# The broadcast matmul of B in a Mamba stage contracts over 128 rows in place of 64

## The chip, the cores and the metric

One core of a Trainium2 chip runs the whole program. The metric is the device time in microseconds (us) of one execution. The kernel before took 3117.87 us (median of 3 runs, 3114.83 to 3124.79).

## The reference, cut to what matters

The model is a chain of residual blocks on `x` of shape (4, 1024, 128), float32: a mixture of experts, a Mamba block, the same mixture again, a ternary feed-forward, an attention, the ternary again. Only the Mamba block is touched. Each of its two directions computes

```python
xz = h @ in_proj_w.T
x, z = (xz[..., :D_INNER], xz[..., D_INNER:])
x = jax.nn.silu(_causal_depthwise_conv(x, conv_w, conv_b))
x_dbl = x @ x_proj_w.T
dt = jax.nn.softplus(x_dbl[..., :DT_RANK] @ dt_proj_w.T + dt_proj_b)
Bm = x_dbl[..., DT_RANK:DT_RANK + D_STATE]
Cm = x_dbl[..., DT_RANK + D_STATE:]
dA = jnp.exp(dt[..., None] * A)
dBx = (dt * x)[..., None] * Bm[:, :, None, :]
h = dA_t * h + dBx_t            # step by step in time
y = jnp.einsum('bdn,bn->bd', h, C_t)
```

with D_INNER = 256 channels and D_STATE = 16 states. For each state n, one row of Bm (a value for each time step) is needed on all 128 partitions, since it multiplies `dt * x` of every channel.

## The kernel before, in words

The function `mamba` works in 16 blocks `b` of 512 time steps: 4 sequences, 2 directions, 2 halves of a sequence. A block has 16 steps `v`, one for each state, and each step handles two halves `h` of 128 channels, so 512 pairs (called G) in all. For one pair:

- ACT makes `dA` = exp(dt * A) (line 1446), in a ring of 8.
- PE makes `Bp`, the row of B of this state on all partitions, once for the two halves (`rows`, line 1276). The stationary operand is `sel[:, v, :]`, zeros and ones that pick the row, and the moving operand is `bcs`, which holds B and C in 64 rows: rows 0 to 31 the part that was rounded off, rows 32 to 63 the rounded value, both float32r. So the matmul contracts over 64 rows. `Bp` is a ring of 3 PSUM banks, and a bank is free again when the scans of its step are done.
- DVE multiplies `u` = dt * x by `Bp` (line 1551) and runs the scan (line 1527) into `H`.
- POOL multiplies `H` by C (`cb`, which a DMA brings) into `hc` (line 1634), a ring of 8.
- PE adds `hc` into `Y` by a matmul with the identity in float32 (line 1339, two instructions for each pair).

Each engine has its own list of instructions, written out in this order. On PE a step `v` issues `rows(b, v + 2)`, then at most one of the projections that use the bank `O` (`o_use`: T transposes at 1288, x at 1294 to 1296, which is 12 matmuls, z at 1299 to 1301, xp at 1305, dt at 1309, out at 1314), then `add_y(b, v - 1)`. `uses_of` says which projection comes at which step. At `v = 1` `add_y` also opens `Y` for the block (`open_y`, lines 1329 and 1331). The projections of a block prepare the next or the one after it: dt goes over ACT (`softplus`) and POOL (lines 1660, 1656, 1651) to `u` (line 1645), which DVE needs at the first product of a block.

Before the scans, in block -1, DVE copies the selection matrix to `sel` (line 1589) out of `dA`, where a DMA put it, and then normalizes the second group of rows (line 1497). PE waits for `s_pre` before the first `rows`.

Of the kernel before, what the change touches and what calls it, by code (L numbers as in the profile page):

```python
# [8 lines left out]
F32R = mybir.dt.float32r  # L9
ACT = mybir.ActivationFunctionType  # L10
ALU = mybir.AluOpType
AX = mybir.AxisListType.X

P = 128
# [3 lines left out]
BLK = 512  # L18
# [5 lines left out]
def wait(eng, sem, value):  # L24

    if not isinstance(value, int) or value > 0:
        eng.wait_ge(sem, value)
# [18 lines left out]
class Phase:  # L46
# [5 lines left out]
    def sb(self, name, shape, dt=F32):  # L52
        return self.ctx.enter_context(self.nc.sbuf_tensor(f"{self.tag}_{name}", shape, dt))
# [4 lines left out]
    def sem(self, name):  # L58
        s = self.ctx.enter_context(self.nc.semaphore(f"{self.tag}_{name}"))
        self.sems.append(s)  # L60
        return s
# [1028 lines left out]
def mamba(nc, tag, x, ident, w, back):  # L1090

    NS = 16
    DBC = 2 * 2 * NS
# [8 lines left out]
    RING = 4  # L1102
# [5 lines left out]
    def place(b):  # L1108

        return b // 4, (0, 0, 1, 1)[b % 4], (0, 1, 1, 0)[b % 4]  # L1110

    def has_scan(b):
        return 0 <= b < NB
# [40 lines left out]
    def through(what, b, v):  # L1154

        return sum(k in COUNTED[what] for bb, vv, k in ORDER if (bb, vv) <= (b, v))

    def slot_of(b, lag, kind):

        use = lambda v: uses_of(b).get(v - lag)  # L1160
        return lambda v: use(v) if use(v) and use(v)[0] == kind else None

    with ExitStack() as ctx:
        ph = Phase(nc, ctx, tag)
        sb, sem = ph.sb, ph.sem
# [5 lines left out]
        dtw = sb("dtw", [DBL, 2, HALF, P])  # L1171
        alog, aneg = sb("alog", [P, 2, HALF, NS]), sb("aneg", [P, 2, HALF, NS])
        wo = sb("wo", [P, HALF, P])
        sel = sb("sel", [DBC, NS, P], F32R)
        mhalf, one, mone = sb("mhalf", [P, TILES]), sb("one", [P, 1]), sb("mone", [P, 1])
        pads = sb("pads", [P, PADW])
        stats, mv = sb("stats", [P, TILES, 6]), sb("mv", [P, TILES, 2])
# [3 lines left out]
        zs = sb("zs", [P, HALF, NCH, BLK])  # L1181
        xs = sb("xs", [P, 4, HALF, BLK])
        dbl = sb("dbl", [DBL, 2, BLK])
        bcs = sb("bcs", [DBC, 4, BLK], F32R)
        dt, u = sb("dt", [P, 2, HALF, BLK]), sb("u", [P, 2, HALF, BLK])
        ROUNDS = UB // RING
        HW = BLK + ROUNDS
# [1 line left out]
        H, hc = sb("H", [P, RING, HW]), sb("hc", [P, HCRING, BLK])  # L1189
# [11 lines left out]
        O = ph.ps("O", [P, BLK])  # L1201
# [4 lines left out]
        s_cst, s_aexp, s_wh, s_wc, s_wl, s_pre = (sem(n) for n in ("cst", "aexp", "wh", "wc", "wl", "pre"))  # L1206
# [4 lines left out]
        s_O, s_Od, s_Oa = sem("O"), sem("Od"), sem("Oa")  # L1211
# [2 lines left out]
        s_ab, s_ee, s_uu, s_ln, s_um = sem("ab"), sem("ee"), sem("uu"), sem("ln"), sem("um")  # L1214
        s_sr, s_co = sem("sr"), sem("co")
        s_dt, s_u = sem("dt"), sem("u")
        s_B = sem("B")
        s_cb = [sem(f"cb{r}") for r in range(RING)]
        s_dA, s_bx, s_scan = sem("dA"), sem("bx"), sem("scan")
# [11 lines left out]
        sels = dA[0:DBC, 0:RING, :].rearrange("p a (n c) -> p (a n) c", c=P)  # L1231
# [15 lines left out]
        def padded(c, shift=0):  # L1247
            return slice(PADW + c * BLK + shift, PADW + (c + 1) * BLK + shift)

        with nc.Block() as block:  # L1250
# [16 lines left out]
            def _(pe):  # L1267
                def rows(b, v):

                    Q = b * NS + v  # L1270
                    if Q >= NB * NS:
                        return
                    if Q % NS == 0:
                        pe.wait_ge(s_bcs, Q // NS + 1)
                    wait(pe, s_scan, 2 * (Q - BRING) + 2)
                    pe.matmul(Bp[:, Q % BRING, :], sel[:, Q % NS, :], bcs[:, Q // NS % 4, :], start=True, stop=True)\  # L1276
                      .then_inc(s_B, 1)

# [86 lines left out]
            def _(act):  # L1365
# [13 lines left out]
                def o_read(b, v, use):  # L1379
                    kind, part, tb = use  # L1380
                    i, e, c = place(tb)
                    if kind == "out":
                        return
                    act.wait_ge(s_O, through("O", b, v))
                    if kind == "T":
                        act.activation(xh[:, padded(c)], O[:], ACT.Copy).then_inc(s_xh, 1)
                    elif kind == "x":
                        act.activation(xs[:, tb % 4, part, :], O[:], ACT.Copy).then_inc(s_Oa, 1)
                    elif kind == "z":
                        wait(act, s_g, 4 * i)  # L1390
                        act.activation(zs[:, part, c, :], O[:], ACT.Copy).then_inc(s_Oa, 1)
                    elif kind == "xp":
                        wait(act, s_crow, 16 * tb)
                        act.activation(dbl[:, tb % 2, :], O[0:DBL, :], ACT.Copy).then_inc(s_dbl, 1)
                        act.activation(bcs[:, tb % 4, :], O[0:DBC, :], ACT.Copy).then_inc(s_Oa, 1)
                    else:
                        m = 2 * tb + part
                        bias = vecs[:, 1, e, part:part + 1]
                        act.activation(ab[:], O[:], ACT.Abs, bias=bias).then_inc(s_ab, 1)
                        wait(act, s_dt, m - 1)  # L1400
                        act.activation(rl[:, part, :], O[:], ACT.Relu, bias=bias).then_inc(s_Oa, 1)
# [74 lines left out]
            def _(dve):  # L1476
                ch = Chain(dve, s_gch)

                def returned(b):
                    back.combine(dve, ring, s_read, x, b, ch)  # L1480
# [28 lines left out]
                def product(G):  # L1509
                    return bx[:, G // 2 % 2, :] if G % 2 == 0 else Bp[:, G // 2 % BRING, :]  # L1510
# [29 lines left out]
                for b in range(-1, NB + 1):  # L1540
                    uses = uses_of(b)
                    for v in range(NS):
                        if has_scan(b):
                            for h in range(HALF):
                                G = b * UB + 2 * v + h
                                dve.wait_ge(s_B, b * NS + v + 1)
                                if G == UB:
                                    scan(G - 1)
                                if G % UB == 0:
                                    dve.wait_ge(s_u, 2 * (b + 1))  # L1550
                                dve.tensor_tensor(product(G), u[:, b % 2, h, :], Bp[:, G // 2 % BRING, :],  # L1551
                                                  ALU.mult).then_inc(s_bx, 1)
                                if G not in (0, UB):
                                    scan(G - 1)
                            if G == NB * UB - 1:
                                scan(G)
                        if (b, v) in RETURNS:
                            n, group = RETURNS[b, v]
                            returned(n)
                            if group:  # L1560
                                statistics(GROUPS[group])
                        if v == 1 and b > 0 and (b - 1) % 4 in (2, 3):
                            gate(b - 1)
                        if b > 0 and slot_of(b, -2, "T")(v):
                            normalize(uses[v + 2][2])
                        if slot_of(b, 2, "T")(v):
                            c = place(uses[v - 2][2])[2]
                            dve.wait_ge(s_xh, through("D", b, v - 2) - sum(
                                k == "out" for bb, vv, k in ORDER if (bb, vv) <= (b, v - 2)))
                            dve.tensor_tensor(xl[:, padded(c)], O[:], xh[:, padded(c)].bitcast(F32), ALU.subtract)\  # L1570
                               .then_inc(s_Od, 1)
                        if slot_of(b, 2, "out")(v):
                            i, _, c = place(uses[v - 2][2])
                            dve.wait_ge(s_O, through("O", b, v - 2))
                            xb = x[:, i * SEQ + c * BLK:i * SEQ + (c + 1) * BLK]
                            dve.tensor_tensor(xb, xb, O[:], ALU.add).then_inc(s_Od, 1)
                        if (b, v) == (-1, 3):
                            returned(1)
                            statistics(GROUPS[1])
                            dve.wait_ge(s_ld, 16 * len(LOADS))  # L1580
                            for e in range(2):
                                for h in range(HALF):
                                    last = dve.tensor_scalar(diag[:, e, h, :], ident[:], vecs[:, 2, e, h:h + 1], None,
                                                             ALU.mult)
                            last.then_inc(s_pre, 1)
                            dve.wait_ge(s_aexp, 1)
                            dve.tensor_scalar(aneg[:], aneg[:], -1.0, None, ALU.mult).then_inc(s_pre, 1)
                            dve.wait_ge(s_sel, 16)
                            dve.tensor_copy(sel[:], sels).then_inc(s_pre, 1)
                            normalize(1)  # L1590

            @block.gpsimd
# [822 lines left out]
```

## Time and profile before

| | |
|---|---|
| median of 3 timed runs | 3117.87 us |
| lowest and highest | 3114.83 and 3124.79 us |
| the profiled execution, span from first to last instruction | 3183.4 us |
| PE / weight loads / DVE / ACT / POOL busy over the span | 83% / 53% / 74% / 55% / 45% |

The profiled execution is slower than the timed ones: its span alone is 65.5 us, or 2.1%, over their median. The page of the profile has no time for the same execution outside the span. The scans of the Mamba block run from about 395 to 1425 us of the span. PEld in a row is the load of weights into the array, and PE the matmul itself. A shape such as 64\*128 in a row of PE is rows times columns of the array that the instruction uses.

### The profile page before, as it was taken

The numbers are of one execution on the slowest core, as the hardware profiler recorded it, in microseconds if no ns is written. First come the engines' busy times: TensorE is split into PE (matmuls) and PEld (weight loads), VectorE is DVE, ScalarE is ACT, GpSimd is POOL, SyncE is SP. The second block draws the span as 40 slices with busy tenths as digits, with TensorE's granted clock in tenths as the row PEclk, the third lists the DMA queues.
The fourth block names the chain that finished last, engine by engine and source line by source line (L and its number), as shares of the span: only waits on it lengthen the run. The fifth ranks groups of instructions, "written<-read, shape, count | busy, mean of one in ns | idle before, by whom it ended". The sixth has DMA issues, their size and how long they took to land. (4 is left out here: it accounts for less than half of the span.)

```text
span 3183.4 us, 38531 instructions
## 1 busy us (share of the span) xinstructions
PE 2649.1 (83%) x11128; PEld 1684.0 (53%) x11128; DVE 2342.8 (74%) x4109; ACT 1746.4 (55%) x3003; POOL 1430.6 (45%) x1514
## 2 busy tenths in 40 slices
PE   6888378889889989867888589949888889885999
PEld 5666233333334334225766467736555556553877
DVE  6688279989999999987688544477878777764444
ACT  3467365546556646523566345536776667763554
POOL 2465578888878878863464440031211111110000
PEclk9899688989899989996899789969999999996999
DMA  2146222222222222211146200000000000001000
GB/s 66 34 131 133 76 62 64 70 64 72 64 70 72 72 67 70 73 57 54 36 134 115 66 26 1 0 12 1 1 1 2 2 1 1 1 1 37 7 7 13
DMA packets 99373, 146.10 MB, mean 46 GB/s; under 512 B 12892, under 2 KB 50524, under 8 KB 98980
## 3 DMA queue, kind: packets, MB, share of 16 engines
q1 hardware_dynamic: 82052, 98.41, 10.5%
q0 software_dynamic: 16608, 44.78, 6.4%
q8 instruction: 91, 1.49, 0.2%
q14 instruction: 110, 0.90, 0.1%
q10 hardware_dynamic: 512, 0.53, 0.1%
HBM read 124.78 MB, written 18.87 MB: 45 GB/s over the span
## 5 line engine op out<-in xcount | busy, mean ns | idle before, releaser
L1634 POOL TENSOR_TENSOR a_hc<-a_H,a_cb 128x512 f32<-128x512 f32 x512 | 622.4, 1226 | 191.0 <-DVE a_H L1527 160.5
L1339 PE MATMUL a_Y<-a_hc,ident 128*128 128x512 f32 x1024 | 533.1, 640 | 36.8 <-POOL a_hc L1634 34.8
L2074 DVE TENSOR_REDUCE a_mx<-a_W 128x1 f32<-128x512 f32 (+3 forms) x768 | 397.2, 550 | 159.0 <-PE a_W L1878 104.7
L1980 ACT ACTIVATE a_pt<-a_W 128x512 f32<-128x512 f32 (+3 forms) x768 | 353.2, 492 | 227.8 <-PE a_W L1891 224.9
L1446 ACT ACTIVATE a_dA<-a_dt,a_aneg 128x512 f32<-128x512 f32 x512 | 339.7, 714 | 207.9 <-DVE a_H L1527 114.8
L1339 PEld LDWEIGHTS a_Y<-a_hc,ident 128*128 128x128 f32 x1024 | 182.7, 196 | 264.7 <-POOL a_hc L1634 134.8
L1891 PE MATMUL a_W<-a_Q,a_K 128*128 128x512 f32 (+3 forms) x768 | 303.2, 400 | 4.4 <-issue 2.3
L2222 POOL TENSOR_TENSOR a_spare<-a_zero 128x1 f32<-128x1 f32 x128 | 27.1, 212 | 582.7 <-ACT a_pt L1980 582.7
L1875 PE MATMUL a_W<-a_K,a_Q 128*128 128x512 f32 (+3 forms) x768 | 274.9, 365 | 10.8 <-DVE a_mx L2074 10.5
L411 ACT ACTIVATE m_raw<-m_U,m_wg 128x512 f32<-128x512 f32 x248 | 173.6, 701 | 127.7 <-PE m_U L306 122.9
L1009 DVE TENSOR_TENSOR t_hl<-t_raw,t_hh 128x512 fp32r<-128x512 f32 x128 | 88.1, 691 | 209.3 <-ACT t_hh L924 184.6
L1551 DVE TENSOR_TENSOR a_bx<-a_u,a_Bp 128x512 f32<-128x512 f32 x256 | 173.7, 678 | 77.6 <-POOL a_u L1645 41.6
L682 POOL DMA_INDIRECT m_xg<-m_xrows,m_gidx x184 | 194.5, 1057 | 70.4 <-issue 54.9
L1891 PEld LDWEIGHTS a_W<-a_Q,a_K 128*128 128x128 f32 x768 | 146.9, 193 | 143.5 <-issue 67.0
L576 DVE TENSOR_TENSOR m_hl<-m_raw,m_hh 128x512 fp32r<-128x512 f32 x248 | 172.3, 695 | 61.0 <-ACT m_hh L415 50.3
L814 PE MATMUL t_U<-t_hh,t_wh 128*128 128x512 f32 x512 | 204.0, 398 | 0.2 <-issue 0.2
L816 PE MATMUL t_U<-t_hl,t_wh 128*128 128x512 f32 x512 | 202.2, 395 | 0.7 <-issue 0.7
L815 PE MATMUL t_U<-t_hh,t_wl 128*128 128x512 f32 x512 | 202.1, 395 | 0.0
L1907 PE MATMUL a_PV<-a_pt,a_V 128*32 128x512 f32 (+3 forms) x1536 | 168.2, 510 | 40.7 <-POOL a_pt L2225 39.7
L1276 PEld LDWEIGHTS a_Bp<-a_bcs,a_sel 64*128 64x128 f32 x256 | 48.4, 190 | 285.2 <-DVE a_H L1527 176.1
L1276 PE MATMUL a_Bp<-a_bcs,a_sel 64*128 64x512 f32 x256 | 130.5, 511 | 79.7 <-DVE a_H L1527 79.4
L923 ACT ACTIVATE t_raw<-t_U,t_scal 128x512 f32<-128x512 f32 x128 | 88.2, 689 | 194.2 <-PE t_U L816 162.5
(311 smaller groups left out, 6432.0 us busy)
## 6 DMA issues: line engine op xcount, KB each, us to landing
a_cb<-a_crow SPq DMA_DIRECT2D x256, 256.0 KB, 3.2
m_orows<-m_yt SPq DMA_DIRECT2D x46, 256.0 KB
t_wst<-ternary_w SPq DMA_DIRECT2D x22, 256.0 KB, 2.9
m_xrows<-m_pool SPq DMA_DIRECT2D x16, 256.0 KB, 2.3
m_xg<-m_xrows,m_gidx POOLq DMA_INDIRECT x184
out<-x SPq DMA_DIRECT2D x8, 256.0 KB, 2.3
m_wg<-moe_ws SPq DMA_DIRECT2D x2, 516.0 KB, 4.4
a_hc<-mamba_conv_rows SPq DMA_DIRECT2D x1, 1024.0 KB
```

Source lines behind the costliest of these rows:

```text
L682: pool.indirect_dma_start(xg[:, j % NXG, t * P:(t + 1) * P], None, xrows, bass.IndirectOffsetOnAxis(ap=gidx[:, n:n + 1], axis=0))\
L814: pe.matmul(out, wh[:, piece, c], rhs_h, start=start, stop=False)
L815: pe.matmul(out, wl[:, piece, c], rhs_h, start=False, stop=False)
L816: return pe.matmul(out, wh[:, piece, c], rhs_l, start=False, stop=stop)
L1276: pe.matmul(Bp[:, Q % BRING, :], sel[:, Q % NS, :], bcs[:, Q // NS % 4, :], start=True, stop=True)\
L1339: pe.matmul(Y[:, h, :], ident[:], hc[:, g % HCRING, :], start=False, stop=v == NS - 1).then_inc(s_y, 1)
L1446: act.activation(dA[:, G % ARING, :], dt[:, b % 2, h, :], ACT.Exp, scale=aneg[:, d, h, v:v + 1]).then_inc(s_dA, 1)
L1634: pool.tensor_tensor(hc[:, G % HCRING, :], H[:, s, span], cb[:, v % RING, :], ALU.mult).then_inc(s_hc, 1)
L1875: mm = pe.matmul(out, Q[:, g * GH + j, tile(t)], K[:, g, c * BLK:c * BLK + cols], start=True, stop=not diag)
L1891: pe.matmul(W[:, 3 + u % 3, 0:BLK - r * P], K[:, g, tile(kt)], Q[:, g * GH + j, c * BLK + r * P:(c + 1) * BLK], start=True, stop=True).the ...
L1980: act.activation(pt[:, u % PR, 0:BLK - r * P], W[:, 3 + u % 3, 0:BLK - r * P], ACT.Exp).then_inc(s_exp, 1)
L2074: dve.tensor_reduce(dst, W[:, s % 3, 0:min(BLK, (t + 1) * P - c * BLK)], AX, ALU.max)\
```

## The change

`sel` and `bcs` get 128 partitions. The matmul of `rows` is given all 128 of both, so it contracts over 128 rows. DVE writes zeros into the lower 64 rows of both once, before the first use, by multiplying 64 partitions of `H` (which POOL has set to zero) by 0.0, and PE waits for the two writes once, before the first `rows`. The rows that carry data are written as before, by the same instructions. The text of the matmul call stays the same; the shape of its operands changes.

```diff
-        sel = sb("sel", [DBC, NS, P], F32R)
+        sel = sb("sel", [P, NS, P], F32R)
...
-        bcs = sb("bcs", [DBC, 4, BLK], F32R)
+        bcs = sb("bcs", [P, 4, BLK], F32R)
...
+        s_rest = sem("rest")
...
                     wait(pe, s_scan, 2 * (Q - BRING) + 2)
+                    if Q == 0:
+                        pe.wait_ge(s_rest, 2)
                     pe.matmul(Bp[:, Q % BRING, :], sel[:, Q % NS, :], bcs[:, Q // NS % 4, :], start=True, stop=True)\
                       .then_inc(s_B, 1)
...
-                        act.activation(bcs[:, tb % 4, :], O[0:DBC, :], ACT.Copy).then_inc(s_Oa, 1)
+                        act.activation(bcs[0:DBC, tb % 4, :], O[0:DBC, :], ACT.Copy).then_inc(s_Oa, 1)
...
-                            dve.tensor_copy(sel[:], sels).then_inc(s_pre, 1)
+                            dve.tensor_copy(sel[0:DBC], sels).then_inc(s_pre, 1)
+                            dve.wait_ge(s_cst, 5)
+                            zeros = H[DBC:P, :, 0:BLK]
+                            dve.tensor_scalar(sel[DBC:P].rearrange("p (a n) c -> p a (n c)", a=RING), zeros,
+                                              0.0, None, ALU.mult).then_inc(s_rest, 1)
+                            dve.tensor_scalar(bcs[DBC:P], zeros, 0.0, None, ALU.mult).then_inc(s_rest, 1)
```

PE, ACT, POOL and SP issue the same instructions in the same order as before. DVE gets two more, in block -1. Before, its list reads there (diag and aneg are constants of the block, a_xn the normalized rows):

```order
L1583 TENSOR_SCALAR a_diag<-ident,a_vecs 128x128 x4
L1587 TENSOR_SCALAR a_aneg<-a_aneg 128x64
L1589 CAST a_sel<-a_dA 64x2048
L1497 TENSOR_SCALAR a_xn<-x,a_mv,a_rstd 128x128 x4
L1551 TENSOR_TENSOR a_bx<-a_u,a_Bp 128x512
```

and with the change:

```order
L1586 TENSOR_SCALAR a_diag<-ident,a_vecs 128x128 x4
L1590 TENSOR_SCALAR a_aneg<-a_aneg 128x64
L1592 CAST a_sel<-a_dA 64x2048
L1595 TENSOR_SCALAR a_sel<-a_H 64x2048
L1597 TENSOR_SCALAR a_bcs<-a_H 64x2048
L1500 TENSOR_SCALAR a_xn<-x,a_mv,a_rstd 128x128 x4
L1554 TENSOR_TENSOR a_bx<-a_u,a_Bp 128x512
```

The two writes of zeros stand between the copy of `sel` and the normalization of the second group.

## Rows read from the trace of the kernel before

**Rows 1.** The page: the span, and the group of the broadcast matmul
```profile
span 3183.4 us, 38531 instructions
...
L1276 PE MATMUL a_Bp<-a_bcs,a_sel 64*128 64x512 f32 x256 | 130.5, 511 | 79.7 <-DVE a_H L1527 79.4
```

**Rows 2.** Busy time by stretch: length, then each engine's busy us, granted clock, DMA
```profile
1007.00:1010.40 3.40, 3.40 (x10) 2.62 (x9) 3.40 (x5) 1.51 (x3) 2.42 (x3) 0.50 0.23 72
395.00:1425.00 1030.00, 886.04 (x2049) 370.57 (x2050) 962.01 (x1174) 558.97 (x859) 829.03 (x692) 0.92 0.23 68
...
424.00:448.30 24.30, 24.30 (x66) 11.23 (x64) 24.18 (x30) 17.01 (x26) 19.83 (x18) 1.00 0.26 74
```

**Rows 3.** Waits of DVE and POOL, 395 to 1425 us: total, times, longest
```profile
DVE a_bx L1551 <- POOL a_u L1645: 41.6, 7, 24.0
DVE a_bx L1551 <- PE a_Bp L1276: 35.9, 22, 5.4
DVE a_H L1527 <- PE a_Bp L1276: 4.4, 1, 4.4
...
POOL a_hc L1634 <- PE a_Y L1339: 29.1, 17, 4.8
```

**Rows 4.** Timeline of PE, 1010 to 1018 us: start, duration, instruction, count
```profile
1010.88 1.88 PE L1329 MATMUL a_Y<-a_xs,a_diag 128*128 128x512 f32 x4
1012.60 1.88 PE L1339 MATMUL a_Y<-a_hc,ident 128*128 128x512 f32 x4
1014.40 0.49 PE L1276 MATMUL a_Bp<-a_bcs,a_sel 64*128 64x512 f32 x1
1014.83 1.98 PE L1339 MATMUL a_Y<-a_hc,ident 128*128 128x512 f32 x4
1016.74 0.50 PE L1276 MATMUL a_Bp<-a_bcs,a_sel 64*128 64x512 f32 x1
1017.17 0.49 PE L1294 MATMUL a_O<-a_xh,a_wch 128*128 128x512 f32 x1
1017.51 0.39 PE L1295 MATMUL a_O<-a_xh,a_wcl 128*128 128x512 f32 x1
1017.74 0.39 PE L1296 MATMUL a_O<-a_xl,a_wch 128*128 128x512 f32 x1
```

**Rows 5.** Timeline of the weight loads (PEld), 1016 to 1018 us
```profile
1016.74 0.18 PEld L1276 LDWEIGHTS a_Bp<-a_bcs,a_sel 64*128 64x128 f32 x1 [0.76 <-issue]
1017.28 0.19 PEld L1295 LDWEIGHTS a_O<-a_xh,a_wcl 128*128 128x128 f32 x1
```

**Rows 6.** Timeline of PE in the ternary stage, float32 transposes between float32r matmuls
```profile
1829.57 0.60 PE L856 MATMUL t_T<-ident,t_xn 128*128 128x128 f32 x4
1829.92 0.48 PE L814 MATMUL t_U<-t_hh,t_wh 128*128 128x512 f32 x1
1830.24 0.39 PE L815 MATMUL t_U<-t_hh,t_wl 128*128 128x512 f32 x1
```

**Rows 7.** Timeline at stalls of DVE, start of a block and later
```profile
1003.89 1.12 PE L1309 MATMUL a_O<-a_dbl,a_dtw 72*128 72x512 f32 x2
...
1006.47 0.47 PE L1294 MATMUL a_O<-a_xh,a_wch 128*128 128x512 f32 x1 [1.02 <-ACT a_rl L1401]
...
1014.93 0.69 DVE L1551 TENSOR_TENSOR a_bx<-a_u,a_Bp 128x512 f32<-128x512 f32 x1 [1.53 <-PE a_Bp L1276]
...
714.93 0.69 DVE L1551 TENSOR_TENSOR a_bx<-a_u,a_Bp 128x512 f32<-128x512 f32 x1 [0.53 <-PE a_Bp L1276]
```

**Rows 8.** Timeline before the first scan, DVE and PE
```profile
357.85 2.28 DVE L1538 TENSOR_TENSOR a_wcl<-a_hc,a_wch 128x2048 fp32r<-128x2048 f32 x1
371.96 1.21 DVE L1589 CAST a_sel<-a_dA 64x2048 fp32r<-64x2048 f32 x1
383.45 1.65 PE L1276 MATMUL a_Bp<-a_bcs,a_sel 64*128 64x512 f32 x3
399.23 0.70 DVE L1551 TENSOR_TENSOR a_bx<-a_u,a_Bp 128x512 f32<-128x512 f32 x1 [24.00 <-POOL a_u L1645]
```

## The prediction

> **What bounds the kernel now.** I read the page first, for the size of the group that changes: 256 broadcast matmuls of 64 by 128, mean 511 ns, 130.5 us busy in all [rows 1]. Then the busy times of the scans, 395 to 1425 us: DVE 962.01 of 1030 us, PE 886.04, POOL 829.03, at a mean granted clock of 0.92 [rows 2]. DVE is the bound, at 93%, so what the change is worth is what it takes out of DVE's idle time. The waits of the same stretch say what that is [rows 3]: 35.9 us in 22 waits and 4.4 us in one for the broadcast matmul, together **40.3 us in 23 stalls**, and 41.6 us in 7 for `u` from POOL, of which 24.0 is the wait for the first scan. So at most 40.3 us hang directly on the changed instruction, and 41.6 - 24.0 = 17.6 us on a chain that begins with a matmul (dt) and passes ACT and POOL. PE has the rest of its time to spare: whatever is saved while DVE is not waiting is worth nothing.
>
> **What a broadcast matmul costs PE now.** The timeline shows it where PE is never idle [rows 4]. Full-size float32r matmuls start 0.23 us apart (1017.51 to 1017.74). The broadcast at 1016.74 is followed by the next matmul 0.43 us later: 0.20 more. That next one takes 0.34 to its successor (1017.17 to 1017.51): 0.11 more. And the way in costs too: four full-size float32 instructions that another full-size one follows last 1.72 us (1010.88 to 1012.60), four that a broadcast follows last 1.80 (1012.60 to 1014.40), 0.08 more, and with a broadcast on both sides 1.91 (1014.83 to 1016.74). The sum is 0.20 + 0.11 + 0.08 = **0.39 us per broadcast**, about 100 us over 256 of them. The weight loads show how: the load of the broadcast starts at 1016.74, together with its matmul, while that of L1295 starts at 1017.28, 0.23 before its matmul [rows 4, 5]. The load of the broadcast is not made ahead.
>
> Is it the rows, or the change from float32 to float32r? In the ternary stage float32 transposes of full size stand between float32r matmuls. Four transposes take 0.35 us and the first matmul behind them 0.32 to its successor [rows 6], 0.67 in all. A float32 instruction of 512 columns takes 1.72 / 4 = 0.43 [rows 4], so a transpose of 128 columns 0.11 and four 0.43; with 0.23 for the float32r matmul that is 0.66, the same. A change of type costs nothing there. What is left is the 64 rows. No row shows this matmul with 128. The page TensorEngine Tiling (Array Packing) of the Trainium skill says under Key Properties that changing the tiling mode drains the TensorE; by that rule all of the 0.39 us goes.
>
> **The sum.** With all 128 rows I take the broadcast as any other full float32r matmul, 0.23 us, with its load ahead. The bounds of the saving per broadcast are 0 (the penalty belongs to something else) and 0.39. What of it reaches DVE:
>
> - *Stalls behind a run that begins with x* (6 of the 23). The one at 1014.93 is 1.53 us [rows 7]. PE's run back from it begins at 1006.47, released by ACT, which had waited for the dt matmuls at 1003.89; they stand right behind a broadcast and would end 0.31 us sooner. The granted clock is 0.50 from 1007.00 to 1010.40 [rows 2], so the 12 matmuls of x last 4.4 us (1006.47 to 1010.88 [rows 4]) and not 12 x 0.23 = 2.8. One entry into a broadcast, 0.08, ends the run. 0.4 us each: 2.4 us.
> - *Stalls behind a run that begins with the opening of Y* (7). No broadcast lies in the run except the last. 0.1 each: 0.7 us.
> - *Short stalls with three broadcasts in the run* (3, each 0.53 as at 714.93 [rows 7]). Two whole penalties lie ahead, 0.78: gone, 1.6 us.
> - *The remaining 7*, of them one of 4.4 us in the first block [rows 3], the others short. Ahead of that one PE is busy for 24.30 of 24.30 us [rows 2], with 7 broadcasts: 7 x 0.39 = 2.7, and a little for the others: 3 us.
> - *The six waits for u* after the first, 17.6 us. POOL stands 29.1 us in 17 waits for PE's `add_y` [rows 3], and these get shorter. Between 0 and 17.6 us; I take 0.5 each, near the low end, because POOL is held by DVE's scans far oftener: 3 us.
>
> 2.4 + 0.7 + 1.6 + 3 + 3 = 10.7, so **11 us**.
>
> *Added.* Two writes of 64 x 2048 by DVE. The nearest row is the copy to `sel` of the same size, 1.21 us; above it a 128 x 2048 subtraction, 2.28 [rows 8]. So 2.4 to 4.6 us. DVE is free at 371.96 + 1.21 = 373.17, so the writes end at 375.6 to 377.7, and the normalization (four small instructions) stands behind them. PE first reads `sel` at 383.45 and the normalized rows after that, and DVE itself has 24.00 us idle before 399.23, which it spends on POOL's chain to `u`, in which no DVE instruction stands [rows 8]. Cost 0; without that cover it would be 2.4 to 4.6 us once. The one new wait of PE passes at once for the same reason. The moving operand reads 64 more partitions, in the same number of columns.
>
> The profiled execution is 3183.4 us, 65.5 over the median, and I take the saving over unchanged: 3183.4 - 11 = 3172 there, and 3117.87 - 11 = **3107 us**, 0.35% faster.
>
> **The rivals.** A measurement of this kernel can tell about 0.3% from no change, 9.4 us; the line to "faster" is 3108.5.
>
> 1. *Nothing reaches DVE, or the penalty stays.* For it: 13 of the 23 stalls have one broadcast, at the very end, and begin with a wait for ACT; what sets their length is the half clock in the run and the 4 + 4 float32 instructions of opening and adding. If the drain belongs to this matmul for another reason than its rows (the ring of three PSUM banks, say), nothing changes at all. Against: no other float32r matmul shows it. Gives 3115 to 3120, say 3118. A rule of the Trainium skill speaks for this side: TensorE: Matmul & The Clock Gate, LDWEIGHTS and the table at its end, has the cost of a matmul and of its load set by columns alone, the same for 32 rows as for 128. By it the time would be 3118. The 0.39 us in the rows is what that rule leaves out.
> 2. *More than the sum.* PE gets 100 us back where it had 1030 - 886 = 144 spare. If the stalls come from backlog that I have not followed past the last wait, most of the 40.3 go, and part of the 17.6. With three quarters of the first and a quarter of the second: 30 + 4 = 34, 3084. Against: the runs as read.
> 3. *Slower, by the clock.* The granted clock is 1.00 (2.4 GHz) in most of the stretch and 0.50 (1.2 GHz) for short times, such as 1007.00 to 1010.40; with PE always busy from 424.00 to 448.30 it was 1.00 [rows 2]. A PE that finishes its work sooner stands idle longer between steps, and the bubbles around the broadcast may be what keeps it counted as busy. A fall costs at most 40.3 / 23 = 1.75 us, if each stall comes from one. It takes 11 / 1.75, 7 more falls, to eat the gain and (11 + 9.4) / 1.75, 12, to be 0.3% slower; with 14 it is 3117.87 - 11 + 24.5 = 3131. Against: the columns that PE streams per step stay the same.
>
> **How the numbers follow.** The sum as it stands 0.52, rival 1 0.20, rival 2 0.17, rival 3 0.11. The likeliest gives 3107; its own range is 3099 to 3114, from half of the terms to them all with the upper ends of the last two. Seven in ten of it lie under 3108.5: 0.36, with 0.17 of rival 2 and little else: faster 0.53. Same: 0.16 + 0.20 + 0.02 of rival 3 = 0.38. Slower 0.09. The range goes from 3085, which leaves half of rival 2 out, to 3124, which leaves out most of rival 3.
>
> **What would show it.** In the profile after, the broadcast reads 128\*128. Its load starts some 0.2 us before its matmul where PE is never idle; the next matmul starts 0.23 us after it and not 0.43; four `add_y` instructions between two broadcasts last 1.72 us and not 1.91. PE's busy time from 395 to 1425 us falls by up to 100 us. DVE's waits for `Bp` fall from 40.3 to about 32 us, those of 0.53 us are gone, those for `u` fall from 17.6 to about 15, and the mean clock stays near 0.92. It is wrong if the load still starts with its matmul (rival 1), if DVE's waits for `Bp` fall under 20 us (rival 2), or if the clock falls below 0.90 (rival 3).

## The result and the profile after

| | before | after |
|---|---|---|
| median of the timed runs, us | 3121.33 (4 runs) | 3099.2 (4 runs) |
| lowest and highest | 3114.83 to 3126.7 | 3097.39 to 3105.92 |
| ratio, 95% interval | | 0.9932 [0.9915, 0.995] |

The median of 3117.87 us given for the kernel before was that of three of the four runs. A second set of runs, below, gave 0.995 [0.9937, 0.9963]. The change makes the kernel 0.5 to 0.7% faster, by 22 us in the first set and 18 in the second; 3107 us was forecast, 11 us less than 3117.87. So the measured saving is between 1.6 and 2 times the one that was forecast.

The page after, span and the group of the broadcast, to be set beside [rows 1]:

```profile
span 3103.9 us, 38534 instructions
...
L1279 PE MATMUL a_Bp<-a_bcs,a_sel 128*128 128x512 f32 x256 | 175.9, 689 | 114.5 <-DVE a_H L1530 114.0
```

The mean of one broadcast rose from 511 to 689 ns, and yet PE has less to do. The timeline of PE shows why the mean misleads (start, duration, instruction, count), to be set beside [rows 4]:

```profile
982.13 1.88 PE L1332 MATMUL a_Y<-a_xs,a_diag 128*128 128x512 f32 x4
983.84 1.88 PE L1342 MATMUL a_Y<-a_hc,ident 128*128 128x512 f32 x4
985.16 0.80 PE L1279 MATMUL a_Bp<-a_bcs,a_sel 128*128 128x512 f32 x1
985.79 1.88 PE L1342 MATMUL a_Y<-a_hc,ident 128*128 128x512 f32 x4
987.11 0.79 PE L1279 MATMUL a_Bp<-a_bcs,a_sel 128*128 128x512 f32 x1
987.74 0.39 PE L1297 MATMUL a_O<-a_xh,a_wch 128*128 128x512 f32 x1
987.97 0.39 PE L1298 MATMUL a_O<-a_xh,a_wcl 128*128 128x512 f32 x1
```

and the weight loads there, beside [rows 5]:

```profile
985.13 0.19 PEld L1279 LDWEIGHTS a_Bp<-a_bcs,a_sel 128*128 128x128 f32 x1 [0.24 <-DVE a_H L1530]
985.56 0.42 PEld L1342 LDWEIGHTS a_Y<-a_hc,ident 128*128 128x128 f32 x2 [0.24 <-issue]
```

At 1.72 us, as full-size ones take [rows 4], the four add_y instructions that start at 983.84 end at 985.56. The broadcast is marked at 985.16, 0.40 us before that, and its load at 985.13: both are now under way while the last add_y is still running, and the length of the broadcast's row counts that overlap. So single marks are not comparable; a whole round is. From broadcast to broadcast with four add_y instructions between, it was 1014.40 to 1016.74, 2.34 us [rows 4], and is 985.16 to 987.11, **1.95**: 0.39 less. The matmul of x behind a broadcast is followed after 0.23, not 0.34.

DVE's waits from the first product to the end of the stage, beside [rows 3]: line, what it waited for, us in total, times, longest.

```profile
DVE a_bx L1554 <- POOL a_u L1653: 40.3, 7, 22.8
DVE a_bx L1554 <- PE a_Bp L1279: 22.4, 11, 5.3
DVE a_H L1530 <- PE a_Bp L1279: 4.5, 1, 4.5
```

The waits for the broadcast fell from 40.3 us in 23 (39.8 in 21 in the second profile before) to 26.9 in 12. Those for `u`, without the first, went from 17.6 to 40.3 - 22.8 = 17.5: nothing. POOL's waits for add_y fell from 29.1 us in 17 [rows 3] (23.4 in 14 in the second profile before) to

```profile
POOL a_hc L1642 <- PE a_Y L1342: 3.8, 8, 0.6
```

The length of the Mamba stage can be read off PE, from its first transpose to the first matmul of the next stage. Before, in a second profile of the unchanged kernel:

```profile
336.07 1.09 PE L1288 MATMUL a_O<-ident,a_xn 128*128 128x128 f32 x4 [27.88 <-DVE a_xn L1497]
...
1413.71 1.08 PE L267 MATMUL m_U<-ident,m_pool 128*128 128x128 f32 x4 [9.06 <-DVE m_pool L464]
```

and after:

```profile
337.00 1.08 PE L1291 MATMUL a_O<-ident,a_xn 128*128 128x128 f32 x4 [27.86 <-DVE a_xn L1500]
...
1400.90 1.09 PE L267 MATMUL m_U<-ident,m_pool 128*128 128x128 f32 x4 [9.17 <-DVE m_pool L464]
```

1077.6 us against 1063.9: 13.7 us, and DVE's waits for the broadcast account for 39.8 - 26.9 = 12.9 of it, both from the same pair of profiles. The first profile before had 3183.4 us of span [rows 1], but its Mamba stage was 1078.2 us by the same marks (356.71 to 1434.86). What was odd in it lies in the other stages, which the change does not touch. The profiled execution after, 3105.92 us, was the slowest of its four, 6.7 us over their median, so its stage need not show all of the 22 us.

The two writes of zeros took 1.23 and 1.22 us, as the copy to `sel` had, and DVE then stood idle 22.79 us:

```profile
353.42 1.23 DVE L1595 TENSOR_SCALAR a_sel<-a_H 64x2048 fp32r<-64x2048 f32 x1
354.57 1.22 DVE L1597 TENSOR_SCALAR a_bcs<-a_H 64x2048 fp32r<-64x2048 f32 x1
...
379.73 0.70 DVE L1554 TENSOR_TENSOR a_bx<-a_u,a_Bp 128x512 f32<-128x512 f32 x1 [22.79 <-POOL a_u L1653]
```

### The profile page after: what moved, and what is told of

Read it like the earlier page. It is cut to its first block and busy times, and to the rows that moved or that the text cites. A ratio compares the mean times of both kernels' runs of the same rounds, so it can differ in the third digit from the quotient of the medians.

```text
span 3103.9 us, 38534 instructions
## 1 busy us (share of the span) xinstructions
PE 2567.3 (83%) x11128; PEld 1677.9 (54%) x11128; DVE 2345.7 (76%) x4111; ACT 1751.3 (56%) x3003; POOL 1426.2 (46%) x1514
## 5 line engine op out<-in xcount | busy, mean ns | idle before, releaser
L1279 PE MATMUL a_Bp<-a_bcs,a_sel 128*128 128x512 f32 x256 | 175.9, 689 | 114.5 <-DVE a_H L1530 114.0
L1554 DVE TENSOR_TENSOR a_bx<-a_u,a_Bp 128x512 f32<-128x512 f32 x256 | 173.2, 677 | 62.8 <-POOL a_u L1653 40.3
L1915 PE MATMUL a_PV<-a_pt,a_V 128*32 128x512 f32 (+3 forms) x1536 | 166.9, 507 | 41.2 <-POOL a_pt L2233 40.1
```

## The experiments

Three questions: is it the rows, or something that came with them; how many rows does it take, and does the penalty belong to the matmul or to the change of height; and where in a block does the gain reach DVE. All ratios are to the kernel before. Each run has one profile, of one execution, and that one can lie some us off the median of its runs; where it does, the text says so.

### Before and after once more

> The kernel before, unchanged, profiled once more. The first profile had a span 62 us over its own timed median, and its two mixture stages took 342 and 339 us against 322 and 316 in the profile of the change, though the change does not touch them. Expected if that one execution was odd outside the Mamba stage: a span near 3120 us, the mixture stages near 320, and the Mamba stage unchanged at 1078 us, with some 40 us of DVE waiting for the broadcast. Expected if the change acts outside the Mamba stage: the mixture stages near 340 us again.

Measured: 3123.13 us, 1.0005 [0.9996, 1.0015], span 3119.1, with a Mamba stage of 1077.6 us. DVE waited 35.4 + 4.4 us for the broadcast. The odd profile did not come again, and comparisons of stages below are made against this one.

> The changed kernel, unchanged, to narrow its interval. Expected: 0.993 to 0.996 of before (the profiles show 14.3 us less in the Mamba stage, which is 0.995), with DVE's waits for the broadcast near 27 us again and POOL's for add_y near 4 us.

Measured: 3105.5 us, 0.995 [0.9937, 0.9963], span 3089.7. DVE waited 13.3 us in 7 and 4.7 in 1 for the broadcast, not 27 as in the first profile after; POOL's waits for add_y were 5.1 us. The profiled execution, 3091.45 us, was the fastest of its six by 12 us. So one execution of the same kernel loses 27 us there and another 18. What differs is the clock at the starts of the blocks, which the section on the reasons shows.

### The zeros without the rows

```diff
-                    pe.matmul(Bp[:, Q % BRING, :], sel[:, Q % NS, :], bcs[:, Q // NS % 4, :], start=True, stop=True)\
+                    pe.matmul(Bp[:, Q % BRING, :], sel[0:DBC, Q % NS, :], bcs[0:DBC, Q // NS % 4, :], start=True, stop=True)\
```

> All of the change but the matmul: 128-partition sel and bcs, the two writes of zeros and PE's wait, while the broadcast contracts over 64 rows as before. Theory of the mode (the array is emptied around a matmul that uses half of its rows): no gain, 1.000 within 0.2%, broadcast loads start with their matmul as before. Theory that placement or the shift of the start brought the gain: 0.993 to 0.996 as in the change.

Measured: 3125.33 us, 1.0016 [1.0005, 1.0026]. The round with four add_y instructions takes 2.34 us again:

```profile
994.58 0.49 PE L1279 MATMUL a_Bp<-a_bcs,a_sel 64*128 64x512 f32 x1
995.00 1.98 PE L1342 MATMUL a_Y<-a_hc,ident 128*128 128x512 f32 x4
996.92 0.50 PE L1279 MATMUL a_Bp<-a_bcs,a_sel 64*128 64x512 f32 x1
```

The preparation gains nothing; the interval reaches from 1.5 to 8 us of loss. The Mamba stage does not show that loss: it took 1078.0 us against 1077.6, with 40.1 us of waits for the broadcast against 39.8. All of the gain is the matmul's.

### 72 rows in place of 128

```diff
+                    pe.matmul(Bp[:, Q % BRING, :], sel[0:DBL, Q % NS, :], bcs[0:DBL, Q // NS % 4, :], start=True, stop=True)\
```

> The changed kernel, but the broadcast contracts over 72 rows, 64 with data and 8 of zeros. Theory of the mode: all of the gain, 0.993 to 0.996, load ahead of the matmul, four add_y instructions between two broadcasts 1.72 us. Theory that more rows at work keep the clock up: 8 of the 64 added rows, an eighth of the gain, 0.999, and a granted clock as before.

Measured: 3109.98 us, 0.9955 [0.9937, 0.9974], and a round of 1.95 us:

```profile
987.03 0.79 PE L1279 MATMUL a_Bp<-a_bcs,a_sel 72*128 72x512 f32 x1
987.66 1.88 PE L1342 MATMUL a_Y<-a_hc,ident 128*128 128x512 f32 x4
988.98 0.80 PE L1279 MATMUL a_Bp<-a_bcs,a_sel 72*128 72x512 f32 x1
```

With 0.23 for the broadcast, 1.72 us of the round are left for the four add_y, as forecast; the marks show 1.32, since the broadcast is marked 0.40 us ahead of their end. DVE waited 26.2 us for the broadcast, and the granted clock from 395 to 1390 us was 0.94, as after the change. 8 rows of zeros do what 64 do. It is a matter of which side of a step between 64 and 72 rows the contraction lies on, not of how many rows work. A gain by the number of rows, 0.999, lies outside the interval.

### Each broadcast twice

```diff
+                    for twice in range(2):
+                        mm = pe.matmul(Bp[:, Q % BRING, :], sel[:, Q % NS, :], bcs[:, Q // NS % 4, :], start=True,
+                                       stop=True)
+                    mm.then_inc(s_B, 1)
```

> The kernel before with each broadcast issued twice in a row, 64 rows both, the second writes the same values over the first. If the array is emptied on the change between half and full height, the second starts 0.23 us after the first, with its weights loaded ahead, and PE has 256 x 0.23 = 59 us more to do: 10 to 25 us slower. If it is emptied for every 64-row matmul, the second starts 0.43 us after the first, PE has 110 us more and becomes the bound in the first half: 40 us or more slower.

Measured: 3131.55 us, 1.003 [1.0015, 1.0046], 11 us slower. The round is 996.02 to 998.59, 2.57 us, 0.23 more than with one broadcast:

```profile
996.02 0.73 PE L1277 MATMUL a_Bp<-a_bcs,a_sel 64*128 64x512 f32 x2
996.67 1.98 PE L1341 MATMUL a_Y<-a_hc,ident 128*128 128x512 f32 x4
998.59 0.73 PE L1277 MATMUL a_Bp<-a_bcs,a_sel 64*128 64x512 f32 x2
```

So a 64-row matmul behind another costs no more than a full one. The 0.39 us are paid for going to half height and back, once per visit. The Trainium skill (TensorEngine Tiling (Array Packing), Key Properties) has the rule that changing the tiling mode drains the TensorE. The runs agree with it, and put 0.39 us on going there and back at full clock; the draining itself is in no row, only the loads that no longer start ahead and the longer round.

> The changed kernel with each broadcast issued twice in a row over 128 rows: 59 us more of PE, against 100 us that the change had given back. If what counts is PE's time alone, it lands between the changed kernel and the kernel before, 0.996 to 1.000 of before. If the smooth loading ahead counts for itself (the clock), it stays at 0.994.

The same edit on the changed kernel. Measured: 3103.99 us, 0.9933 [0.9911, 0.9955]. The round is 983.50 to 985.69, 2.19 us, 0.24 more than with one broadcast, so PE has some 59 us more to do (an estimate, 256 x 0.23). They cost nothing that can be measured, though they are more than half of what the change gives back. DVE waited 20.2 us for the broadcast. The busy times of a stretch of the scans (its length, the busy us of PE, weight loads, DVE, ACT and POOL, then the clock):

```profile
395.00:1390.00 995.00, 836.76 (x2292) 411.04 (x2290) 948.74 (x1161) 552.27 (x848) 816.47 (x683) 0.96 0.23 69
```

A granted clock of 0.96. The same stretch of the kernel before, in its second profile, has 0.93:

```profile
395.00:1390.00 995.00, 866.07 (x1997) 359.37 (x1996) 938.25 (x1146) 550.69 (x846) 808.17 (x673) 0.93 0.24 69
```

The two profiles of the changed kernel have 0.94 and 0.95 there, and the kernel before with every broadcast doubled has 0.95 too and is 11 us slower, so a higher mean clock is not a gain by itself. Taken alone, this run would also fit a gain in which the first 40 us taken from PE do everything. The runs of the next section speak against that.

### Half of the broadcasts, by parity and by place

```diff
+                    kk = P if Q % 2 else DBC
+                    pe.matmul(Bp[:, Q % BRING, :], sel[0:kk, Q % NS, :], bcs[0:kk, Q // NS % 4, :], start=True, stop=True)\
```

> The changed kernel, but only the broadcasts of odd steps contract over 128 rows, those of even steps over 64. Theory of the mode, with the gain in proportion to the penalties taken from PE: half of it, about 0.9975, PE some 50 us less busy in the Mamba stage than before, DVE waiting some 30 us for the broadcast. Rival (the gain comes from one place alone, the start of a block): all of it or nothing, by whether that broadcast has the 128 rows; the stall stands before the broadcast of step 4, an even one, so then near 1.000.

Measured: 3111.37 us, 0.9959 [0.9946, 0.9973]. DVE waited 31.6 us for the broadcast, near the 30 expected, but the profiled execution, 3116.4 us, was the slowest of its ten. Half of the penalties bring 4/5 of the gain of the second set of runs, or 3/5 of that of the first; the 0.9975 that was expected lies just outside the interval. The rival as it was stated, near 1.000 because step 4 is an even one, is out. That half of the broadcasts bring all of the gain is not excluded: the whole change had 0.995 [0.9937, 0.9963]. The next two split by place, with the condition `Q % NS < 5` and its opposite.

> The changed kernel with 128 rows only in the broadcasts of steps 0 to 4 of each block, 5 of 16, those that PE issues from the end of one block until the stall at the start of the next; 64 rows in the others. If the gain is made at the start of a block, where PE gets to x and to the opening of Y a little sooner and before the clock is halved: nearly all of it, 0.995 to 0.996. If it goes by the number of penalties: 5/16 of it, 0.9985.

Measured: 3107.81 us, 0.9963 [0.9945, 0.9981]. The 0.9985 of proportion lies outside. DVE's waits:

```profile
DVE a_bx L1555 <- PE a_Bp L1280: 15.6, 8, 5.2
DVE a_H L1531 <- PE a_Bp L1280: 4.3, 1, 4.3
```

19.9 us, and POOL's for add_y 5.2 us in 11: as in the full change, with 5 of 16 of the penalties gone. This profile is of the fastest of the seven executions, 3097.64 us, 10 us under their median.

> The opposite: 128 rows in steps 5 to 15, 64 rows in steps 0 to 4. By the start of the block: 0.999 to 1.000, but for the short stalls of 0.53 us and the one in the first block. By the number of penalties: 11/16, 0.9965.

Measured: 3112.96 us, 0.9978 [0.9961, 0.9994]. DVE's waits:

```profile
DVE a_bx L1555 <- PE a_Bp L1280: 26.2, 12, 5.5
DVE a_H L1531 <- PE a_Bp L1280: 4.6, 1, 4.6
```

30.8 us, in an execution 6 us under the median of its runs. Here 11 of 16 penalties take 9 us off the waits, and the other 5 took 20. The intervals of the two times overlap, so the order of the two rests on one profile each, and those lie differently far under their medians. What the times do show is that the five at the start bring more than their share: 0.9985 was outside their interval. For the other eleven the times decide nothing, since both 0.999 and the 0.9965 of proportion lie inside.

The traces say more than the times. In eight of the sixteen blocks, x (12 matmuls) stands on PE right ahead of the opening of Y. In the first two of the eight the granted clock was 0.50 for part of x in every one of the profiles below. In the other six x either had the full clock throughout and lasted 2.85 to 2.87 us, or the half clock for part of it and lasted 4.3 us and more:

| run | with the half clock in x, of 6 | PE busy over the stage, us | Mamba stage, us |
|---|---|---|---|
| before, first and second profile | 5 and 4 | 906.3 and 904.1 | 1078.2 and 1077.6 |
| zeros without the rows | 4 | 904.5 | 1078.0 |
| each broadcast twice, 64 rows | 3 | 947.2 | 1084.3 |
| 128 rows in steps 5 to 15 | 3 | 851.1 | 1068.1 |
| 128 rows in odd steps | 2 | 867.5 | 1068.7 |
| 72 rows | 1 | 840.6 | 1063.2 |
| after, first and second profile | 1 and 0 | 840.4 and 830.6 | 1063.9 and 1054.2 |
| each broadcast twice, 128 rows | 0 | 863.6 | 1057.7 |
| 128 rows in steps 0 to 4 | 0 | 874.7 | 1056.8 |

But for the run that gives PE some 43 us more to do than before, the stage goes with the second column rather than with the third: 128 rows in steps 0 to 4 leave PE 24 us busier than 128 rows in steps 5 to 15, and the stage is 11 us shorter. That is also the answer to a gain that the first 40 us of PE's time would bring. These are single executions, and the clock was never set apart from the rest, so the table shows what goes together.

### The opening of Y moved

Of the stalls that are left, 8 of 12 in the first profile after and 6 of 8 in the second end a run of PE that begins with the matmuls that add D * x, and in the backward direction the other's result, to `Y` (lines 1332 and 1334). These only have to be in the sum before the block ends.

```diff
+    OPEN = 3
...
-                def open_y(b):
+                def free_y(b):
                     i, d, c = place(b)
...
+                def skip_y(b):
+                    i, d, c = place(b)
                     for h in range(HALF):
-                        pe.matmul(Y[:, h, :], diag[:, d, h, :], xs[:, b % 4, h, :], start=True, stop=False)
+                        pe.matmul(Y[:, h, :], diag[:, d, h, :], xs[:, b % 4, h, :], start=False, stop=False)
...
-                                  start=False, stop=v == NS - 1).then_inc(s_y, 1)
+                                  start=v == 0, stop=v == NS - 1).then_inc(s_y, 1)
+                    if v == OPEN:
+                        skip_y(b)
```

> The changed kernel, with the matmuls that add D * x and the other direction's result to Y (4 or 8 float32 instructions, 1.7 to 3.4 us at full clock) moved from the start of a block to after add_y of step 3, where no projection stands. The stalls of DVE that are left (18 to 27 us for the broadcast) begin with these in all but two cases. Expected if they make them: DVE's waits for the broadcast 5 to 12 us, time 0.990 of before. If the half clock alone makes them: as the changed kernel, 0.995.

Measured, on the changed kernel: 3089.49 us, **0.9897 [0.9878, 0.9916]**, the fastest of all: 31 us, 1%, less than before. DVE's waits for the broadcast from the first product on are 5.1 us in 3 and 5.6 in 1; POOL's for add_y 1.4 us: the forecast of the first case. 9.7 of these 10.7 us are the two stalls in the first block, 4.1 and 5.6. The clock in this profile was no better than before (0.917 over the span, against 0.918): with these matmuls out of the way, a half clock hardly reaches DVE behind the first block.

> The kernel before, broadcast over 64 rows, with the same move of the D * x matmuls to after step 3. If those make the stalls, and the 128 rows are worth something only because DVE waited there, this one alone comes near the other (0.990 to 0.993), with 5 to 12 us of waits for the broadcast. If the 64 rows cost on their own account, it stays behind it by what the change was worth, at 0.995.

Measured, on the kernel before: 3112.9 us, 0.9979 [0.9965, 0.9992]. DVE still waits, in more and shorter stalls, and POOL too:

```profile
DVE a_bx L1557 <- PE a_Bp L1277: 27.7, 29, 3.8
...
POOL a_hc L1640 <- PE a_Y L1343: 33.0, 23, 4.0
```

Neither of the two forecasts. The move alone is worth 0.2%, the rows alone 0.5 to 0.7%, both together 1.0%. That the two help each other is likely but not shown: the move is worth 0.35 to 0.5% on top of the rows, and the intervals leave room for the 0.2% that it has alone. If they do, the rows suggest why: PE with 64 rows has too little slack to take the moved matmuls later without falling behind again.

## Why the prediction was right, and where its sizes were off

**The cost per broadcast** was right to the hundredth: 0.39 us of the round, gone whole, as 1.95 against 2.34 us shows. That it is the rows and not the type was read from the ternary stage [rows 6]; the run with 72 rows and the one with two broadcasts in a row bear it out. Three of the signs given for it were wrong. The load still starts with the mark of its matmul (985.13 and 985.16), which by its letter was the sign of rival 1; the marks of the broadcast and of the next matmul are 0.63 us apart, not 0.23; and the marks around four add_y instructions are 1.32 apart, not 1.72. All three come from one thing, the mark moved ahead with the load, and 0.63 + 1.32 is the 1.95 that 0.23 + 1.72 gives. The period was the thing to name.

**Added work at nothing**: right as far as the Mamba stage goes. The writes ended with 22.79 us of DVE idle behind them, and the stage with them alone was 1078.0 us against 1077.6. The whole program with them alone was 5 us slower, with 1.5 to 8 in the interval; where those lie, no trace shows.

**The sum was 11 us; the stage gave 13.7 in the profile after and 23.4 in the second one** (span 3089.7, stage 1054.2 us by the same marks). The terms, one by one:

- *Stalls behind a run that begins with x*, forecast 0.4 each, 2.4 us. They gave 8.9 us, from 16.7 to 7.8. This is the step that failed. I held the half clock fixed where it was, "the granted clock is 0.50 from 1007.00 to 1010.40 [rows 2], so the 12 matmuls of x last 4.4 us", and took off only what the broadcasts cost. But whether the clock falls there changed. The start of the same block, after, has the clock at full all through x:

```profile
979.28 0.47 PE L1297 MATMUL a_O<-a_xh,a_wch 128*128 128x512 f32 x1 [0.97 <-ACT a_rl L1404]
...
982.13 1.88 PE L1332 MATMUL a_Y<-a_xs,a_diag 128*128 128x512 f32 x4
```

2.85 us for x, not 4.41, and the stall of 1.53 us [rows 7] is not there at all. It is no chance of one execution: x of this block lasts 4.41 or 4.42 us in both profiles before and in the one of the zeros without the rows, and 2.85 or 2.87 in both after and in the one with 72 rows. One block earlier in the same execution the clock was at half when x began, and the stall is there, 2.50 us:

```profile
922.20 0.77 PE L1297 MATMUL a_O<-a_xh,a_wch 128*128 128x512 f32 x1 [1.02 <-ACT a_rl L1404]
...
926.93 1.88 PE L1332 MATMUL a_Y<-a_xs,a_diag 128*128 128x512 f32 x4
...
930.80 0.69 DVE L1554 TENSOR_TENSOR a_bx<-a_u,a_Bp 128x512 f32<-128x512 f32 x1 [2.50 <-PE a_Bp L1279]
```

x took 4.73 us there. Of the six stalls of this kind, 16.7 us together, two were left in the first profile after, 7.8 us with the one in the first block, and that one alone, 5.7 us, in the second. So two executions of the changed kernel differ by 9 us of waits.
- *Stalls behind the opening of Y*, 0.1 each, 0.7 us: 14.7 us in 7 before (and 0.2 in one more), 14.4 in 8 in the first profile after, as small a gain as forecast, and 7.6 in 6 in the second. The move of the opening on the changed kernel took them away.
- *The short stalls of 0.53 us*: gone, as forecast. So are five of the remaining seven, 2.6 us together, but for one of 0.18; I had put them at next to nothing.
- *The first block*: 3 us forecast; the wait of 4.4 us [rows 3] is 4.5 now. Nothing. PE had stood idle for 4.05 us, waiting for ACT, before the run that ends in this stall, and now it stands 6.74: the 2.7 us of the seven penalties went into that wait. I had counted the penalties ahead of the stall past the point where PE itself had been waiting.
- *The waits for u*: 3 us forecast, 17.6 to 17.5. Nothing. POOL's waits for add_y fell by 25 us (by 20 against the second profile before), and none of it reached `u`.

So the missing 6 us of these two terms were more than made good by the first, 6.5 us over its forecast, and by the short stalls. That 11 came as near to 13.7 as it did is in part luck: two terms that gave nothing stood against one that was nearly four times too small. The cost of the broadcast, the bound and the direction were right. Two readings beside the sum were wrong as well: the 1.75 us called the most that a fall of the clock costs is the mean of stalls that reach 5.4, and the lower end of the likeliest's own range, 3099, is not what its terms give; with 4.4 us for the first block and all 17.6 us of the waits for `u` they come to 26.7 us, 3091. Rival 2 (the waits fall much further) turned out half true in the second profile, 18.0 us of waits where it asked for less than 20, but that is the fastest of six executions, and the times, 3099 and 3105.5, stay far above its 3084. Rival 1 is out by the 72 rows and by the round of 1.95 us. Its rule, that rows do not count for a matmul's time (TensorE: Matmul & The Clock Gate of the Trainium skill, LDWEIGHTS and the closing table), holds for the matmul alone, as the second of two 64-row broadcasts shows with 0.23 us, and not for its neighbours. Rival 3, a lower clock, did not come: over 395 to 1425 us the clock was 0.92 [rows 2] and 0.93 in the second profile before, and the changed kernel has

```profile
395.00:1425.00 1030.00, 835.26 (x2132) 386.63 (x2132) 972.35 (x1275) 563.63 (x864) 825.07 (x699) 0.93 0.23 69
```

and 0.94 in its second profile. The bubbles around the broadcast were not what kept it up. PE is 51 us less busy in that stretch, where I had said up to 100. The stretch holds 2132 matmuls after and 2049 before, though; over the whole stage, with 2097 in both, PE's busy time fell from 906.3 to 840.4 us, by 66. No run splits the rest.

**What stays open.** Why the clock keeps up at those starts. The run with 72 rows shows that it is not the number of rows at work; the run with 128 rows in steps 0 to 4, with the full clock in x at all six, points at the five broadcasts around the start. That PE, with dt and x behind those broadcasts, has its work nearer together there would fit both, but no run set that apart. Nor do the profiles say where the rest of the timed gain lies in the first set of runs (22 us against 13.7 in the stage); the profiled execution was the slowest of its four, which may account for 6.7 us of it. In the second set it is the other way round, 18 us against 23.4 in the stage, and the profiled execution was 14 us under the median.

## What to carry to other kernels

A matmul over 64 rows between full ones costs more around it than in it: here 0.39 us per visit on top of its own 0.23, with the weights of the matmul loaded only when it starts. If the data allows, rows of zeros beyond the 64 (8 were enough here) take it away, and several half-height matmuls in a row pay it once. Read such a cost from the period of a repeating group: the mean of the one instruction rose here while its cost fell. Such a saving is worth only what reaches the engine that bounds the kernel, and it is worth more where PE's lateness coincides with a half clock; there, also look at what can be moved from the crowded step to an empty one, which was worth another 0.35 to 0.5% here.

## What the runs showed that I had not expected

- More work for PE did not cost time: the changed kernel with every broadcast doubled, 59 us more, was at 0.9933 [0.9911, 0.9955], with a granted clock of 0.96 in the stretch of scans, against 0.93. The same doubling over 64 rows cost 11 us.
- The mark of a matmul in the profile moves with its weight load: 689 ns in place of 511 for an instruction that had become cheaper.
- A span 62 us over the kernel's own median in one profiled execution, with the examined stage unchanged at 1078 us.
